# Conditioned residual stack on one core: the first eight turns of the first convolution in halves, a second queue for two transfers and a store, attention spread by row tiles

## The chip, the cores and the metric

One core of a Trainium2 chip. The time is the device time of one launch in microseconds (us), the median over runs; every run is the whole kernel. TensorE (PE) multiplies, ScalarE (ACT) and VectorE (DVE) work elementwise, GpSimd (POOL) copies, SyncE (SP) issues most of the transfers.

## What is computed

Four layers, each added to its input, on `x` of 32 samples x 128 channels x 2048 positions:

```python
x = x + conv9(x, weight0, groups=4, pad=4) + (c @ cw0.T)[:, :, None] + side[:, None]
x = x + einsum('boi,bih->boh', att1 @ experts1, x) + (att1 @ bias1)[:, :, None]
x = x + einsum('boi,bih->boh', att2 @ experts2, x) + (att2 @ bias2)[:, :, None]
x = x + conv9(x, weight3, groups=4, pad=4) + (c @ cw3.T)[:, :, None] + side[:, None]
# att = softmax(gelu(gelu(c @ W0 + b0) @ W1 + b1) @ W2 + b2), 8 experts of 128 x 128
```

## The kernel before

One sample at a time goes through three stages on TensorE. The two mixing layers have nothing nonlinear between them, so their two matrices are multiplied into one per sample (the *product*). A convolution over 2048 positions is laid out in four phases (`PH`) of 512 positions; with 9 taps this makes `SHIFTS` = 12 shifted products. Each fp32 value is split in a high and a low part in the matmul's own format, and three of the four partial products are summed, so a convolution has `TURNS` = 36 turns. A turn is four matmuls side by side (L836), one for each of the four groups of 32 channels, each in its own row tile of TensorE and with its own PSUM bank: turns 0 to 11 are high x high, 12 to 23 low taps, 24 to 35 low data. `conv0` is the first convolution, `mix` the mixing (12 turns, L906), `conv3` the last one, `product` the small matmul of the two matrices (L886, L893).

In the steady state, for each sample: ScalarE adds the bias and writes the high part (`high_y` L465, `high_z` L475), VectorE writes the low part (`low_y` L630, `low_z` L640), VectorE sums the expert matrices with the attention of the sample (`mix_matrices`, 16 instructions of L669), splits the product in `prod` (`split_product`, L677 to L682), and SyncE spreads it by four transfers of 32 partitions each to the four row blocks of `mix_w` (`spread_mix_w`, L326). GpSimd reorders the input and the output.

The order of the work on every engine is written out by hand; engines meet by semaphores only. The part that the change touches is the start and the end:

- **TensorE, start** (from L996 on). 12 filler matmuls (`keep_busy`, L998), the transpose of the condition (L1005), 4 fillers, the transpose of the five bias rows (L1008), 2 fillers, `hidden(0)` (L981: first MLP layer of both attentions), then `conv0(zero)` in groups of turns, and between the groups: `hidden(1)`, `logits` (L991, L992), transposes of the context weights (L1018), `mix2_transposes(0)` (L943: four expert matrices of the second mixer, to bank 4), `contexts` (L962), the attention's transposes (L1025), the broadcast of the attention of all samples to all partitions (L1030: a matmul of ones in 32 rows and a table `spread` of 32 x 512), `mix2_transposes(1)` to bank 5, the second mixer's attention bias (L1038), `conv_biases` (L969), the mixed bias in ten matmuls (`mixed_bias`, L955), the product of sample 0 after turn 24. Then turns 0 to 15 of the convolution of sample 1, and `mix(zero)`, which waits for all of `y_lo` and for the four transfers to `mix_w`.
- **ScalarE, start.** Six transfers (L550 to L554), the gelu table, the high parts of the taps (L489), the copy of the columns (L568), the gelus (L495), the exponentials (L574), the copies of the transposes (`mix2_transposed`, L500), the first planes of sample 1 (L455), the bias table (L590, L598), `high_y(zero)`.
- **VectorE, start.** Transpose of the taps (L689), high part of sample 0 (L771), low parts of the taps (L697), low part of sample 0 in pieces (`low_direct`, L621), softmax (L781 to L788), `spread` (L790), context columns (L751), copy of the attention table (L801), mixed terms (L805), the matrices.
- **The end.** The last sample's second convolution is done in two halves of 256 columns (`last_conv`, L874). VectorE transposes it to positions (L728, L731), VectorE or ScalarE adds the bias (L738, L533). ScalarE interleaves sample 30 (`weave_half`, L542). SyncE issues the stores of the last sample in eight pieces (L378) and that of sample 30 in two (L371), in the order: half 0 of groups 2, 3, 0, 1; the two of sample 30; half 1 of groups 0 to 3. A wait on SyncE holds all that stands behind it.

## Time and profile before

| | us |
|---|---|
| median of 3 runs (662.95 to 663.0) | 663.0 |
| the profiled execution | 663.23 |
| its span on the core | 661.4 |
| TensorE matmuls busy | 650.6 (98%) |
| VectorE busy | 476.5 (72%) |
| ScalarE busy | 262.3 (40%) |
| GpSimd busy | 241.7 (37%) |

The span runs from the first to the last recorded instruction; what the profiled execution has beyond it lies around it. An instruction on an engine starts when the one before it on the same engine has started and its semaphores allow it; a chain of waits is read backwards from the last instruction.

### The profile page before, as it was taken

The numbers are of one execution on the slowest core, as the hardware profiler recorded it, in microseconds if no ns is written. First come the engines' busy times: TensorE is split into PE (matmuls) and PEld (weight loads), VectorE is DVE, ScalarE is ACT, GpSimd is POOL, SyncE is SP. The second block draws the span as 40 slices with busy tenths as digits, with TensorE's granted clock in tenths as the row PEclk, the third lists the DMA queues.
The fourth block names the chain that finished last, engine by engine and source line by source line (L and its number), as shares of the span: only waits on it lengthen the run. The fifth ranks groups of instructions, "written<-read, shape, count | busy, mean of one in ns | idle before, by whom it ended". The sixth has DMA issues, their size and how long they took to land.

```text
span 661.4 us, 24661 instructions
## 1 busy us (share of the span) xinstructions
PE 650.6 (98%) x11220; PEld 595.9 (90%) x11220; DVE 476.5 (72%) x945; ACT 262.3 (40%) x328; POOL 241.7 (37%) x85
## 2 busy tenths in 40 slices
PE   8999999999999999999999999999999999999994
PEld 6889999999999999999999999999999999999994
DVE  7898867687767677677677677677677677677635
ACT  4643424433424433424433423433423433433434
POOL 3024334433424433434443433442433442433220
PEclk9999999999999999999999999999999999999998
DMA  7355776454566455566455566545566545444515
GB/s 235 97 162 161 224 224 213 155 175 183 168 222 219 153 168 191 159 222 222 156 163 194 154 222 222 165 153 199 150 223 223 164 154 205 153 154 161 159 67 192
DMA packets 50325, 118.77 MB, mean 180 GB/s; under 512 B 5557, under 2 KB 26090, under 8 KB 42474
## 3 DMA queue, kind: packets, MB, share of 16 engines
q1 hardware_dynamic: 49602, 117.48, 54.7%
q8 instruction: 28, 0.46, 0.3%
q10 hardware_dynamic: 488, 0.69, 0.3%
q14 instruction: 15, 0.12, 0.1%
q0 software_dynamic: 192, 0.02, 0.0%
HBM read 35.33 MB, written 33.55 MB: 104 GB/s over the span
## 4 chain that ended last, share of the span: by engine, by line
PE 96%; DVE 1%; DMA 1%; SPq 0%; ACTq 0%; ACT 0%; issue 0%
PE ps L836 79%; PE ps L906 14%; PE ps L893 1%; DMA out_planes<-in_L_cond_b 1%; PE ps L874 1%; DVE x_in L728 1%; DMA mix_w<-prod 1%; DVE x_planes L731 0%; PE ps L955 0%; SPq L326 0%; PE ps L943 0%; ACTq L554 0%; ACT x_planes L533 0%; PE ps L981 0%; PE ps L886 0%
## 5 line engine op out<-in xcount | busy, mean ns | idle before, releaser
L399 POOL COPY out_sb<-out_planes 128x2048 f32<-128x2048 f32 x30 | 118.7, 3956 | 220.4 <-DVE mat2T L669 208.4
L390 POOL COPY x_planes<-x_in 128x2048 f32<-128x2048 f32 x29 | 112.7, 3887 | 137.8 <-DVE x_lo L616 137.8
L465 ACT ACTIVATE y_hi<-ps,bias_tab 128x512 fp32r<-128x512 f32 x128 | 77.5, 689 | 189.1 <-PE ps L836 189.1
L640 DVE SCALAR_TENSOR_TENSOR z_lo<-ps,bias_tab,z_hi 128x1024 fp32r<-128x1024 f32 x62 | 76.8, 1280 | 69.2 <-ACT z_hi L475 69.2
L630 DVE SCALAR_TENSOR_TENSOR y_lo<-ps,bias_tab,y_hi 128x512 fp32r<-128x512 f32 x128 | 87.3, 745 | 38.9 <-ACT y_hi L465 38.9
L836 PE MATMUL ps<-z_hi,taps_lo 32*128 32x512 f32 x1488 | 99.4, 397 | 0.0
L836 PE MATMUL ps<-x_hi,taps_hi 32*128 32x512 f32 x1536 | 97.2, 391 | 0.0
L836 PE MATMUL ps<-x_hi,taps_lo 32*128 32x512 f32 x1536 | 96.5, 389 | 0.0
L836 PE MATMUL ps<-x_lo,taps_hi 32*128 32x512 f32 x1536 | 96.0, 390 | 0.0
L836 PE MATMUL ps<-z_hi,taps_hi 32*128 32x512 f32 x1488 | 92.9, 391 | 0.0
L483 ACT ACTIVATE out_taps<-ps,bias_tab 128x512 f32<-128x512 f32 x62 | 39.3, 684 | 134.3 <-PE ps L836 134.3
L836 PE MATMUL ps<-z_lo,taps_hi 32*128 32x512 f32 x1488 | 92.5, 390 | 0.0
L906 PE MATMUL ps<-y_hi,mix_w 32*128 32x512 f32 x1024 | 89.8, 389 | 0.3 <-DMA mix_w<-prod 0.3
L836 PEld LDWEIGHTS ps<-x_hi,taps_hi 32*128 32x128 f32 x1536 | 82.4, 184 | 7.1 <-issue 0.4
L836 PEld LDWEIGHTS ps<-x_lo,taps_hi 32*128 32x128 f32 x1536 | 82.2, 183 | 7.1
L836 PEld LDWEIGHTS ps<-x_hi,taps_lo 32*128 32x128 f32 x1536 | 82.4, 183 | 6.7 <-issue 0.2
L836 PEld LDWEIGHTS ps<-z_hi,taps_hi 32*128 32x128 f32 x1488 | 79.9, 183 | 7.0
L836 PEld LDWEIGHTS ps<-z_lo,taps_hi 32*128 32x128 f32 x1488 | 80.0, 183 | 6.7
L475 ACT ACTIVATE z_hi<-ps,bias_tab 128x1024 fp32r<-128x1024 f32 x62 | 65.7, 1112 | 50.0 <-PE ps L906 50.0
L836 PEld LDWEIGHTS ps<-z_hi,taps_lo 32*128 32x128 f32 x1488 | 77.0, 184 | 5.7
L616 DVE TENSOR_TENSOR x_lo<-x_planes,x_hi 128x2048 fp32r<-128x2048 f32 x31 | 70.8, 2284 | 0.0
L650 DVE TENSOR_SCALAR out_taps<-ps,bias_tab 128x512 f32<-128x512 f32 x62 | 43.7, 747 | 23.2 <-PE ps L836 23.2
(122 smaller groups left out, 554.2 us busy)
## 6 DMA issues: line engine op xcount, KB each, us to landing
x_in<-in_x SPq DMA_DIRECT2D x31, 1024.0 KB, 5.2
out_planes<-out_taps SPq DMA_DIRECT2D x122, 256.0 KB, 2.5
out<-out_sb SPq DMA_DIRECT2D x30, 1024.0 KB, 4.5
mix_w<-prod SPq DMA_DIRECT2D x128, 128.0 KB, 3.6
x_in<-in_x SPq DMA_DIRECT2D x2, 512.0 KB, 5.4
out<-x_planes SPq DMA_DIRECT2D x8, 128.0 KB, 2.1
out<-out_sb SPq DMA_DIRECT2D x2, 512.0 KB, 3.5
out_taps<-in_L_cond_weight SPq DMA_DIRECT2D x1, 512.0 KB, 6.5
```

What stands on the lines that cost most here:

```text
L390: pool.tensor_copy(x_planes[:, :, :], planes(x_in[t.par(d)], slice(0, S))).then_inc(x_planed, 1)
L399: pool.tensor_copy(out_sb[t.par(d)][:, :].rearrange("c (s p) -> c p s", p=PH), out_planes[:, :, :])\
L465: act.activation(y_hi[:, g, :], ps[:, bank(t, 0) + g, :], ACT.Identity, bias=bias_tab[:, b, g:g + 1]).then_inc(y_hi_done, 1)
L475: act.activation(z_home(t, 0)[0][:, 2 * h:2 * h + 2, 1:S + 1], ps[:, k:k + 2, :], ACT.Identity, bias=bias_tab[:, b, 2 * G:BIAS]).then_inc( ...
L483: act.activation(out_taps[:, g, :], ps[:, bank(t, d) + g, :], ACT.Identity, bias=bias_tab[:, b, G + g:G + g + 1]).then_inc(out_act, 1)
L616: dve.tensor_tensor(out=x_lo[p][:, :, 1:S + 1], in0=x_planes[:, :, :], in1=x_hi[p][:, :, 1:S + 1].bitcast(F32), op=ALU.subtract).then_inc( ...
L630: dve.scalar_tensor_tensor(out=y_lo[:, g, :], in0=ps[:, bank(t, 0) + g, :], scalar=bias_tab[:, b, g:g + 1], in1=y_hi[:, g, :].bitcast(F32) ...
L640: dve.scalar_tensor_tensor(out=z_home(t, 0)[1][:, 2 * h:2 * h + 2, 1:S + 1], in0=ps[:, k:k + 2, :], scalar=bias_tab[:, b, 2 * G:BIAS], in1 ...
L650: dve.tensor_scalar(out_taps[:, g, :], ps[:, bank(t, d) + g, :], bias_tab[:, b, G + g:G + g + 1], None, ALU.add).then_inc(out_dve, 1)
L728: dve.transpose(blocks(last_mid[:, h, g, :]), taps).then_inc(last_turned[h], 1)
L836: tile = pe.matmul(ps[:, first_bank + g, :], w[rows(g), d, :], a[rows(g), d % PH, d // PH:d // PH + S], start=(n == 0), stop=(n == TURNS - 1))
L906: tile = pe.matmul(ps[:, bank(t, 0) + p, :], w[rows(p), g, h, :], a[rows(p), g, :], start=(n == 0), stop=(n == 3 * G - 1))
```

## The change

- `half_turns(h, turns)` is new: a group of turns of the first convolution on 256 of the 512 columns. Turns 0 to 7 of sample 0 are done first for the left half (turns 0 and 1, then the transpose of the bias rows, then 2 to 7), which wait only for the left half of `x_hi` and for the taps of their own phase, then, behind `hidden(1)`, for the right half. Four filler matmuls go; the condition column and the bias columns get a copy and a semaphore each.
- The attention is computed on 128 partitions (each sample's logits four times over), both softmaxes share one reciprocal and one multiplication; `spread` has 128 x 128 elements, each block of 32 partitions with 8 samples of its own, and four matmuls of 128 columns, one for each row tile, write 128 columns each of banks 4 to 7. They wait for ScalarE's copy of bank 4. The attention's transpose moves from TensorE and ScalarE to VectorE. Both attention biases are one matmul (`MIXED` is 9).
- On TensorE the small matmuls stand at other places between the turns, the product of sample 0 comes after turn 33, and `mix(zero)` after 18 turns of sample 1.
- ScalarE issues two of the four transfers of sample 0's `mix_w` (`spread_first`), ahead of `high_y(zero)`; one of the four high tap copies of the last convolution moves behind `high_y(zero)`; the planes of sample 1 move behind the second transposes.
- At the end ScalarE issues the second half of sample 30 (`store_woven`), SyncE the first half, third in its line.

```diff
-MIXED = K + 2
+MIXED = K + 1
+SAMPLES = N // G
...
-        ones = sb("ones", [GC, C])
+        ones = sb("ones", [C, C])
+        own_samples = sb("own_samples", [C, SAMPLES])
...
-            spread_mix_w(zero, 0)
+
+            spread_mix_w(zero, 0, range(2))
             load_x(zero, 2)
...
+            store_group(0, 2)
+            store_group(0, 3)
+
+            sp.wait_ge(halves_woven, 1)
+            sp.dma_start(out[N - 2, :, 0:L // 2].rearrange("(g o) x -> o g x", g=G), out_sb[0][:, 0:L // 2])\
+              .then_inc(out_stored[0], DMA)
+            store_group(0, 0)
+            store_group(0, 1)
+            for g in range(G):
+                store_group(1, g)
...
+            def spread_first():
+
+                act.wait_ge(prod_hi_done, 1)
+                act.wait_ge(prod_lo_done, 1)
+                for p in range(2, PH):
+                    act.dma_start(mix_w[0][rows(p), :, :, :].rearrange("o g h z -> o g (h z)").bitcast(F32),
+                                  prod[:, :, :].rearrange("m h z -> m (h z)").bitcast(F32))\
+                       .then_inc(mix_w_spread[0], DMA)
...
+            def store_woven():
+
+                act.wait_ge(halves_woven, 2)
+                act.dma_start(out[N - 2, :, L // 2:L].rearrange("(g o) x -> o g x", g=G), out_sb[0][:, L // 2:L])\
+                   .then_inc(out_stored[0], DMA)
...
+            act.wait_ge(condT_psum, 1)
+            act.activation(condT, ps[:, 6, 0:N], ACT.Copy).then_inc(condT_done, 1)
             for p in range(PH):
                 taps_high(0, p)
-            act.wait_ge(condT_psum, 2)
-            act.activation(mlp_col[:, :], ps[:, 6, 0:N + 5], ACT.Copy).then_inc(condT_done, 1)
+            act.wait_ge(mlp_cols_psum, 1)
+            act.activation(mlp_col[:, N:N + 5], ps[:, 6, N:N + 5], ACT.Copy).then_inc(mlp_cols_done, 1)
             gelus(0)
             gelus(1)
...
             mix2_transposed(0)
-            act.wait_ge(attT_psum, 1)
-            act.activation(attT_sb[:, :, :], ps[0:K, 6, 256:320].rearrange("k (l n) -> k l n", l=2), ACT.Copy)\
-               .then_inc(attT_done, 1)
-            plane_x1(0)
             mix2_transposed(1)
             act.wait_ge(agg_psum, 1)
             act.activation(agg[:, :], ps[:, 6, 320:320 + N], ACT.Copy).then_inc(agg_done, 1)
+            plane_x1(0)
             plane_x1(1)
...
-            for p in range(PH):
+            for p in range(PH - 1):
                 taps_high(1, p)
...
             act.wait_ge(bias_tab_done, 3)
+            spread_first()
             high_y(zero)
+            taps_high(1, PH - 1)
             high_z(zero)
...
             weave_half(0)
             weave_half(1)
+            store_woven()
             bias_last()
...
-            turn_taps(1)
             dve.wait_ge(x_hi_done, 1)
-            low_direct(0, half(0), slice(0, 2), False)
+            low_direct(0, half(0), slice(0, 1))
+            low_direct(0, half(1), slice(0, 1))
             dve.wait_ge(logits_psum, 1)
...
+            turn_taps(1)
+            dve.wait_ge(exp_done, 2)
+            dve.reciprocal(att_inv, att_sum).then_inc(att_inv_done, 1)
...
+                              in0=att.rearrange("c (a k) -> c a k", a=1).to_broadcast([C, SAMPLES, ATT]),
+                              in1=own_samples[:, :].rearrange("c (m a) -> c m a", a=1).to_broadcast([C, SAMPLES, ATT]),
                               op=ALU.mult).then_inc(spread_done, 1)
...
+            dve.transpose(attT_sb[:, :], att_block).then_inc(attT_done, 1)
+            dve.wait_ge(att_tab_psum, G)
+            dve.tensor_copy(att_tab[:, :, :].rearrange("c (r m) k -> c r (m k)", r=G),
+                            ps[:, G:2 * G, 384:512]).then_inc(att_tab_done, 1)
+            for p in range(1, PH):
+                low_direct(0, half(0), slice(p, p + 1))
+                low_direct(0, half(1), slice(p, p + 1), p == PH - 1)
...
+            def half_turns(h, turns):
+
+
+                for n in turns:
+                    if h == 0:
+                        pe.wait_ge(x0_half_hi, 1)
+                        pe.wait_ge(taps_hi_done[0], min(n, PH - 1) + 1)
+                    else:
+                        pe.wait_ge(x_hi_done, 1)
+                    s = n // PH + HALF * h
+                    for g in range(G):
+                        pe.matmul(ps[:, g, HALF * h:HALF * h + HALF], taps_hi[0][rows(g), n, :],
+                                  x_hi[0][rows(g), n % PH, s:s + HALF], start=(n == 0 and h == 0), stop=False)
...
+            def spread_attention():
+
+                pe.wait_ge(spread_done, 1)
+                pe.wait_ge(mix2T_done, 1)
+                for r in range(G):
+                    pe.matmul(ps[:, G + r, 384:512], ones[rows(r), :], spread[rows(r), :, :].rearrange("n m k -> n (m k)"),
+                              start=True, stop=True).then_inc(att_tab_psum, 1)
...
-            keep_busy(4)
-            pe.wait_ge(mlp_rows_in, 5 * DMA)
-            pe.transpose(ps[:, 6, N:N + 5], mlp_rows, ident[0:5, 0:5]).then_inc(condT_psum, 1)
             keep_busy(2)
             hidden(0)
-            pe.wait_ge(taps_hi_done[0], PH)
-            conv0(zero, range(4))
+            half_turns(0, range(2))
+            pe.wait_ge(mlp_rows_in, 5 * DMA)
+            pe.transpose(ps[:, 6, N:N + 5], mlp_rows, ident[0:5, 0:5]).then_inc(mlp_cols_psum, 1)
+            half_turns(0, range(2, 8))
             hidden(1)
-            conv0(zero, range(4, 7))
+            half_turns(1, range(8))
             logits()
...
-            conv0(zero, range(7, 10))
+            conv0(zero, range(8, 11))
             mix2_transposes(0)
-            contexts()
...
+            spread_attention()
             conv0(zero, range(11, SHIFTS))
             pe.wait_ge(taps_lo_done[0], PH)
-            conv0(zero, range(SHIFTS, 14))
+            conv0(zero, range(SHIFTS, 15))
+            contexts()
             mix2_transposes(1)
...
+            conv0(zero, range(15, 19))
             conv_biases()
-            conv0(zero, range(14, 19))
+            conv0(zero, range(19, 25))
             for k in range(MIXED // 2):
                 mixed_bias(k)
-            conv0(zero, range(19, 25))
+            conv0(zero, range(25, 31))
             for k in range(MIXED // 2, MIXED):
                 mixed_bias(k)
+            conv0(zero, range(31, 34))
             product(zero, 0)
-            conv0(zero, range(25, TURNS))
+            conv0(zero, range(34, TURNS))
...
-            conv0(first, range(16))
+            conv0(first, range(18))
             mix(zero)
-            conv0(first, range(16, TURNS - 4))
+            conv0(first, range(18, TURNS - 4))
```

## Rows read from the trace of the kernel before

**Rows 1.** The page: TensorE's granted clock by slice; the ended-last chain by line.

```profile
PEclk9999999999999999999999999999999999999998
...
PE ps L836 79%; PE ps L906 14%; PE ps L893 1%; DMA out_planes<-in_L_cond_b 1%; PE ps L874 1%; DVE x_in L728 1%; DMA mix_w<-prod 1%; DVE x_planes L731 0%; PE ps L955 0%; SPq L326 0%; PE ps L943 0%; ACTq L554 0%; ACT x_planes L533 0%; PE ps L981 0%; PE ps L886 0%
```

**Rows 2.** The chain in order of time, steady part and last convolution: start, us, what.

```profile
83.63 4.20 PE ps L836 x72
...
644.26 4.30 PE ps L874 x143
```

**Rows 3.** The same chain, around the first mixing.

```profile
27.68 3.48 DMA mix_w<-prod
...
31.29 3.07 PE ps L906 x38
```

**Rows 4.** Timeline of TensorE, start: start, us, engine, line, count.

```profile
8.63 0.55 PE L981 MATMUL ps<-mlp_col,out_sb 128*128 128x32 f32 x4
9.11 1.22 PE L836 MATMUL ps<-x_hi,taps_hi 32*128 32x512 f32 x16
...
13.61 0.66 PE L943 MATMUL ps<-ident,out_taps 128*128 128x128 f32 x4
14.11 0.53 PE L962 MATMUL ps<-mlp_col,out_sb 128*128 128x32 f32 x4
...
15.06 0.69 PE L1030 MATMUL ps<-spread,ones 32*128 32x512 f32 x1
...
20.98 1.44 PE L836 MATMUL ps<-x_hi,taps_lo 32*128 32x512 f32 x20
...
22.58 0.85 PE L955 MATMUL ps<-out_sb,mix_wT 128*128 128x32 f32 x6
...
23.92 0.49 PE L886 MATMUL ps<-mat2T,mat 128*128 128x128 f32 x2
```

**Rows 5.** The line that issues the first MLP weights (L346), with its landing.

```profile
L346 SPq DMA_DIRECT2D out_sb<-in_L_cond_W x2: 432/521/610, 1.7 to 2.1; - x2
...
DMA to landing us min/median/max: 5.3/5.4/5.5
```

**Rows 6.** Timeline of the other engines, start, with the idle time before.

```profile
14.31 0.60 ACT L500 ACTIVATE mix_wT<-ps 128x512 f32<-128x512 f32 x1 [0.61 <-PE ps L943]
...
18.82 0.62 DVE L805 TENSOR_TENSOR out_sb<-agg,att_tab 128x256 f32<-128x256 f32 x1 [0.73 <-ACT agg L586]
...
25.03 0.29 DVE L682 TENSOR_TENSOR prod<-prod_sum,prod 128x128 fp32r<-128x128 f32 x1
...
25.41 2.87 SPq L326 DMA_DIRECT2D mix_w<-prod  x4
...
27.25 2.42 ACT L465 ACTIVATE y_hi<-ps,bias_tab 128x512 fp32r<-128x512 f32 x4 [2.15 <-PE ps L836]
28.04 2.73 DVE L630 SCALAR_TENSOR_TENSOR y_lo<-ps,bias_tab,y_hi 128x512 fp32r<-128x512 f32 x4 [0.61 <-ACT y_hi L465]
```

**Rows 7.** The line of the mix_w issues (L326), whole span: ns min/median/max.

```profile
L326 SPq DMA_DIRECT2D mix_w<-prod x128: 547/603/1748, 25.4 to 621.1; - x128
```

**Rows 8.** Timeline of the end: ScalarE and SyncE's issues.

```profile
645.90 1.45 ACTq L521 DMA_DIRECT2D out_planes<-out_taps  x2
...
650.38 3.93 ACT L542 ACTIVATE out_sb<-out_planes 128x1024 f32<-128x1024 f32 x2 [0.91 <-DMA out_planes<-out_taps]
...
652.16 2.53 SPq L378 DMA_DIRECT2D out<-x_planes  x4
...
654.52 0.96 ACT L533 ACTIVATE x_planes<-x_planes,bias_tab 128x256 f32<-128x256 f32 x2 [0.22 <-DVE x_planes L731]
654.74 1.25 SPq L371 DMA_DIRECT2D out<-out_sb  x2
...
656.03 3.34 SPq L378 DMA_DIRECT2D out<-x_planes  x4
656.39 0.96 ACT L533 ACTIVATE x_planes<-x_planes,bias_tab 128x256 f32<-128x256 f32 x2 [0.91 <-DVE x_planes L731]
```

146 lines of the change are left out of this document (74 added, 72 removed).

## Prediction, made before the changed kernel had run

> **What bounds the kernel now.** I read the page first: TensorE at its full clock in every slice but the last, and a chain that ended last which is convolution and mixing matmuls almost to the end [rows 1]. Then the chain in order of time. From about 32 us on it is one unbroken row of TensorE work: 18 turns (72 matmuls) take 4.20 us, 0.233 us a turn, and the turns of 256 columns of the last sample take 4.30 us for 36, 0.119 us each [rows 2]. Nothing of the change touches that middle. What it can move is when TensorE gets into that row, and what comes behind its last matmul. At the start the one piece of the chain that isn't TensorE's is the transfer of the first product to `mix_w`, issued at 27.68 and landed 3.48 us later; `mix(zero)` starts at 31.29 [rows 3]. Ahead of it TensorE is never idle for long, but a lot of its time goes to small matmuls between groups of turns [rows 4]. At the end SyncE issues ten stores in a row, the last four behind the woven sample's two [rows 8].
>
> **First convolution, start.** Now `hidden(0)` starts at 8.63 behind a wait for the five bias rows, and the turns at 9.11, 0.48 us later [rows 4]. In the change `hidden(0)` needs the condition column (cut loose from the bias rows) and its weights; these are issued up to 2.1 and land 5.3 to 5.5 us later, by 7.7 at the latest [rows 5]. The two turns after it need one half of `x_hi` only, which VectorE has by about then. So the turns start at about 7.7 + 0.05 + 0.48 = 8.2 us: 0.9 us earlier. The four filler matmuls that go lay in this wait and cost nothing; nothing else covered it.
>
> **From the first turn to the product.** Before: 9.11 to 23.92, 14.81 us [rows 4]. The change puts 34 turns ahead of the product where 25 stood: 9 x 0.233 = +2.10. The eight in halves cost 8 x (2 x 0.119 - 0.233), +0.04. A group of turns costs more than its turns: six turns from 20.98 to the next small matmul at 22.58 are 1.60 us where 6 x 0.233 = 1.40, and the small matmul ahead of a group waits some 0.08 more, so 0.28 a group. Seven groups (turns 0-3, 4-6, 7-9, 10, 11-13, 14-18, 19-24) become nine (first halves of 0-1 and of 2-7, second halves, 8-10, 11-14, 15-18, 19-24, 25-30, 31-33): +0.56. The transpose of the bias rows moves in: +0.15. Out go the attention row broadcast through one row tile (a pass of 512 columns shows 0.69 us, there are two, partly beside turns of other tiles; against four tiles of 128 columns side by side I take -0.8), the two attention transposes (-0.15) and one of ten matmul pairs of the mixed bias (six records from 22.58 last 0.85, so about -0.23 a pair) [rows 4]. And there is a **new wait**: the four tiles write to banks 4 to 7, bank 4 holds the first transposes of the second mixer, and ScalarE must have copied them. It started its copy 0.70 us after the transposes started and took 0.60 [rows 4, 6]; TensorE is through with the transposes after 0.50 (13.61 to 14.11) and has, in the new order, neither `contexts` nor the attention transposes to fill in. So it idles 0.70 + 0.60 + 0.05 - 0.50 = 0.85 us, with turns 11 to 14 queued behind. Sum: 14.81 + 2.10 + 0.04 + 0.56 + 0.15 - 1.18 + 0.85 = 17.33; the product starts at 8.2 + 17.3 = 25.5 us.
>
> VectorE isn't what the product waits for: its short softmax (two ops for four, a spread of 128 columns for 512) is done before ScalarE's copy is, it copies the table by 15.7, and with six low-part pieces and the context columns behind it reaches the mixed terms at about 19.4, where it stood at 18.82 before [rows 6]; the matrices are ready 4.8 us later, at 24.2, over a microsecond ahead of the product. Its additions at the start (two memsets, four small copies) lie in its wait for the taps. ScalarE's planes of sample 1 move behind the second transposes and end some 1 us later, with its bias column at about 25.6, just ahead of `conv0(first)`; no cost, but the cover is thin.
>
> **From the product to mix(zero).** Before, the product started at 23.92, its low part was done at 25.32, and SyncE issued the four spreads at 0.72 us each [rows 4, 6]. ScalarE's `y_hi` started at 27.25, and VectorE's last `y_lo` ended at 28.04 + 2.73 = 30.77, 3.52 later [rows 6]. In the change ScalarE issues two of the four, and it does so ahead of `high_y(zero)`: both issues count, `y_hi` is queued behind them, `y_lo` waits for `y_hi`, and `mix(zero)` waits for `y_lo`. With P for the product's start, the low part is at P + 1.40 and two issues of 0.72 end at P + 2.88. Then `y_hi` and `y_lo` take 3.52, and mix starts at P + 6.45 = 31.95. The two shorter lines of transfers land earlier than that: P + 1.49 + 0.87 + 3.5 = P + 5.85 (second issue, landing as in [rows 3]). TensorE itself arrives at P + 0.42 + 0.2 + 20 x 0.233 = P + 5.3, so it idles over a microsecond. Mix starts 31.95 - 31.29 = 0.66 us later than before, with two turns less behind it (-0.47): **start part +0.2 us**. The price of ScalarE's issues isn't shown for this transfer. The nearest row is its own pair at the end, 1.45 us for two [rows 8], and that I take. From below: if they delayed `y_hi` by nothing, the transfers decide, 31.35, and the start part is -0.4. From above: SyncE's longest of the 128 issues took 1.75 us [rows 7]; two such ones add 2.1.
>
> The Trainium skill speaks against splitting these transfers: by its page DMA: Bandwidth & Descriptors (Rules for kernel authors) transfers issued from two engines run on the same 16 DMA engines and nothing but issue time is saved. The trace has the last of the four landing 3.48 us after its own issue with three just ahead of it [rows 3], so issue time is what there is to save here; were it engine time, that would be the fourth rival.
>
> **The end.** Nothing before 652 us moves. SyncE's first four stores run 652.16 to 654.69, the woven pair to 655.99, the last four 656.03 to 659.37, which is 0.81 us more than the first four took [rows 8]. The bias of the last two groups is ready at 656.39 + 0.96 = 657.35, so the last issue could start 657.4, and it starts near 658.8. The change has SyncE issue one woven half third in line, and ScalarE the other after its weave ends at 650.38 + 3.93 = 654.31. ScalarE's first two biases then start 0.5 us later (655.05 for 654.52) and end near 656.0; SyncE issues group 0 at 655.6, 1 at 656.2, 2 at 656.9, 3 at 657.55. That is 1.2 us earlier. If the same 0.81 us of slow issues recurs, it is 0.45. With one store less on its queue I take **-1.0** (bounds -0.45 and -1.3). The third ending is none: were ScalarE's issue to take so long that its last biases slip, the gain would be gone.
>
> **Sum.** +0.2 - 1.0 = -0.8. The profiled execution took 663.23 us (span 661.4 and 1.8 around it) and would take 662.4. The median of the runs is 663.0, 0.2 below it, so the forecast is **662.2 us**, 0.12% less. What a measurement can tell from no change is 0.2%, 1.3 us; so this counts as within.
>
> **Rivals.**
> - *The start pays as well.* ScalarE's issues don't hold up `y_hi`, or the product comes earlier than 25.5 because TensorE's wait for the copy of bank 4 is shorter. Start -0.4, end -1.0: 661.6, just over 0.2% faster. For it: the turns do start 0.9 us earlier. Against: rows of ScalarE's queue show it busy for each issue. Chance 0.24.
> - *The end doesn't pay.* Slow issues recur, or ScalarE's issue delays its biases: end 0 to -0.45, start +0.2: 663.0, within. For it: the 0.81 us has no cause in the rows. Chance 0.18.
> - *ScalarE's issues are held like SyncE's slow ones.* Place: the two spreads ahead of `high_y(zero)`. At 1.5 to 1.75 us each the start part is +1.8 to +2.3; with the end at its lower bound that is +1.4 to +1.8, 664.4 to 664.8, say 664.6 us, slower by over 0.2%. It decides from about 1.5 us an issue. For it: `mix(zero)` has no slack against `y_lo`. Against: median of such issues 0.60 [rows 7], and nothing else loads the queue then. Chance 0.07.
> - *The split saves the transfers nothing.* The last one lands as long after the product's start as before (31.16 - 23.92 = 7.24 us), mix starts at 25.5 + 7.24 + 0.13 = 32.9, the start part is +1.1: 663.1, within. Against: the landing follows its issue by the same 3.5 us though the four came 0.75 us apart. By the skill's rule above it would be likelier than I make it. Chance 0.04.
> - *The forecast*, 0.47.
>
> **How the numbers follow.** The range takes the start from -0.4 (with 0.4 us of error on P on the good side) to +0.9, and the end from -1.3 to -0.45: 660.9 to 663.5; it leaves out most of the third rival and the far end of the first. Faster by over 0.2%: the first rival, 0.25 with the forecast's own edge; slower: 0.07; within: 0.68.
>
> **What would show it.** In the changed profile: `hidden(0)` near 7.8 and the first turns, 256 columns wide, near 8.2; TensorE idle 0.6 to 1.0 us ahead of the four spread matmuls, released by ScalarE's copy; the product near 25.5; two issues on ScalarE of about 0.7 us each, `y_hi` right behind them, and mix(zero) near 31.9 released by VectorE's `y_lo`; from there to the last matmul the same row of turns, shifted by +0.2; the last store issued within 0.3 us of the last bias. I am wrong if the last matmul ends over half a microsecond earlier than before, if mix(zero) is released by a transfer, or if the time from the last matmul to the end isn't about 1 us shorter.

## The result, and the profile after

The changed kernel takes **665.47 us**, the median of 10 runs (664.74 to 667.16); the kernel before beside it 663.13 (10 runs, 662.95 to 663.48). The ratio is 1.0039, interval 1.0031 to 1.0047: slower by 0.4%. The forecast was 662.2 within 660.9 to 663.5, so it is wrong in sign and outside its range. The profiled execution took 666.38 us with a span of 664.4; before, 663.23 and 661.4. In the traces the spans are 664.43 and 661.36, so they explain 3.07 of those 3.15 us.

TensorE at the start, timeline of the changed kernel (start, us, engine, line, count, and the idle time before it with what ended it). It answers to [rows 4]:

```profile
7.66 0.63 PE L1052 MATMUL ps<-mlp_col,out_sb 128*128 128x32 f32 x4 [0.32 <-DMA out_sb<-in_L_cond_W]
8.22 0.66 PE L906 MATMUL ps<-x_hi,taps_hi 32*128 32x256 f32 x9
...
14.63 0.46 PE L1073 MATMUL ps<-spread,ones 32*128 32x128 f32 x5 [0.78 <-ACT mix_wT L531]
...
25.45 0.49 PE L954 MATMUL ps<-mat2T,mat 128*128 128x128 f32 x2
...
32.72 0.50 PE L974 MATMUL ps<-y_hi,mix_w 32*128 32x512 f32 x4 [1.89 <-DMA mix_w<-prod]
```

Up to the product every step is where the working had put it: `hidden(0)` 7.66 (7.7 was said), turns 8.22 (8.2), a pause of 0.78 ahead of the spread attention (0.85), the product at 25.45 (25.5). Then `mix(zero)` starts at 32.72 for the 31.95 of the forecast, and what releases it is a transfer, not VectorE. TensorE stood still for 1.89 us. The other engines in that stretch, for [rows 6]:

```profile
26.97 1.60 ACTq L515 DMA_DIRECT2D mix_w<-prod  x2
28.62 2.42 ACT L483 ACTIVATE y_hi<-ps,bias_tab 128x512 fp32r<-128x512 f32 x4 [3.01 <-issue]
...
26.95 1.34 SPq L339 DMA_DIRECT2D mix_w<-prod  x2
...
29.42 2.73 DVE L669 SCALAR_TENSOR_TENSOR y_lo<-ps,bias_tab,y_hi 128x512 fp32r<-128x512 f32 x4 [0.46 <-ACT y_hi L483]
```

ScalarE's two issues take 1.60 us (1.44 was said), and `y_lo` is through at 29.42 + 2.73 = 32.15. So VectorE's line was read nearly right, 0.2 us late; the transfers' line was not. The chain in order of time (start, us, what), for [rows 3]:

```profile
27.70 4.88 DMA mix_w<-prod
32.72 4.62 PE ps L974 x44
```

The last spread, issued at 27.70, lands 4.88 us later, where the issue at 27.68 of the kernel before landed after 3.48. And the mixing behind it takes 4.62 us for 44 matmuls, where 38 took 3.07 before. The windows of this stretch say why (window, its length, busy time and count of PE, PEld, DVE, ACT and POOL, the granted clock, the busy share of the DMA engines, GB/s):

```profile
28.00:30.00 2.00, 2.00 (x43) 2.00 (x40) 1.54 (x5) 1.38 (x3) 0.00 (x0) 1.00 0.93 179
30.00:32.00 2.00, 0.82 (x16) 0.38 (x8) 2.00 (x4) 1.65 (x3) 0.00 (x0) 1.00 1.17 161
...
33.00:34.00 1.00, 1.00 (x16) 0.96 (x15) 1.00 (x1) 0.00 (x0) 0.00 (x0) 0.65 0.94 393
34.00:35.00 1.00, 1.00 (x16) 0.93 (x15) 1.00 (x4) 0.00 (x0) 0.00 (x0) 0.50 0.39 148
35.00:36.00 1.00, 1.00 (x16) 0.96 (x12) 1.00 (x5) 0.00 (x0) 0.00 (x0) 0.50 0.37 74
36.00:37.00 1.00, 1.00 (x19) 0.95 (x16) 0.44 (x2) 0.00 (x0) 0.00 (x0) 0.64 0.91 377
```

Two things are to be seen. While the four spreads run, the DMA engines are busy the whole time (0.93 and 1.17). And just behind the pause the granted clock falls to 0.50, the lower of TensorE's two levels, for 3.4 us. Before, that never happened ahead of the last matmul. In 3 of the 10 runs the mean granted clock is 0.993 where the others have 0.995 and above, and these three spans are 664.4 to 664.5 against 662.3 to 663.3. So the fall belongs to some executions, the profiled one among them.

The end, ScalarE and SyncE, for [rows 8]:

```profile
648.41 1.46 ACTq L552 DMA_DIRECT2D out_planes<-out_taps  x2
...
653.73 1.60 PE L942 MATMUL ps<-x_lo,taps_hi 32*128 32x256 f32 x48
...
654.67 1.24 SPq L385 DMA_DIRECT2D out<-x_planes  x2
654.84 3.87 ACT L573 ACTIVATE out_sb<-out_planes 128x1024 f32<-128x1024 f32 x2 [2.86 <-DMA out_planes<-out_taps]
...
656.92 0.54 SPq L392 DMA_DIRECT2D out<-out_sb  x1
...
657.50 4.94 SPq L385 DMA_DIRECT2D out<-x_planes  x6
...
658.73 0.62 ACTq L579 DMA_DIRECT2D out<-out_sb  x1
```

ScalarE's weave of sample 30 starts 6.43 us after the reload of that sample is issued; in [rows 8] it was 650.38 - 645.90 = 4.48. SyncE waits for the first half of it before its third store, so the line stands from 655.9 to 656.9, and the new order of stores, which was to end 1 us earlier, doesn't: from the start of the last matmul (655.06, before 652.56) to the end of the span it is 9.4 us, where it was 8.8.

**The ledger of the profiled execution**, from the start of the same matmuls in both traces. At `mix(zero)` +1.43 and, with two turns fewer behind it, -0.47: +0.96. The clock: +1.55, seen as a shift of 2.51 us of every mixing from the second to the last. Behind the last matmul +0.57. Outside the span +0.07 (1.95 for 1.88). Together 3.15. **The ledger of the medians** is another one: span +1.85 (663.05 for 661.2), and +0.5 outside the span, where the kernel before has 1.77 to 2.01 in every run whose span is on record, 1.9 in the median, and the changed one 1.84 to 2.92, median 2.41. So four things had to be tested: the wait for the transfers, the clock, the end, and the time outside the span.

### The profile page after: what moved, and what is told of

The parts are those of the page before. It is cut to its first block, busy times and chain, and to the rows that moved or that the text cites. A ratio compares the mean times of both kernels' runs of the same rounds, so it can differ in the third digit from the quotient of the medians.

```text
span 664.4 us, 24740 instructions
## 1 busy us (share of the span) xinstructions
PE 651.0 (98%) x11248; PEld 563.5 (85%) x11248; DVE 477.8 (72%) x954; ACT 262.7 (40%) x328; POOL 241.4 (36%) x85
## 4 chain that ended last, share of the span: by engine, by line
PE 95%; DMA 2%; ACT 1%; DVE 0%; SPq 0%; ACTq 0%; issue 0%; DVEq 0%
PE ps L890 79%; PE ps L974 14%; PE ps L961 1%; DMA out_planes<-out_taps 1%; DMA out_sb<-in_L_cond_W 1%; DMA mix_w<-prod 1%; ACT out_sb L573 1%; PE ps L906 0%; PE ps L1025 0%; ACT x_planes L564 0%; PE ps L1052 0%; DVE out_taps L689 0%; PE ps L1013 0%; PE ps L954 0%; SPq L356 0%
## 5 line engine op out<-in xcount | busy, mean ns | idle before, releaser
L890 PE MATMUL ps<-x_hi,taps_hi 32*128 32x512 f32 x1504 | 93.3, 390 | 0.0
L890 PEld LDWEIGHTS ps<-x_lo,taps_hi 32*128 32x128 f32 x1536 | 77.6, 183 | 11.6
L890 PEld LDWEIGHTS ps<-x_hi,taps_lo 32*128 32x128 f32 x1536 | 77.7, 183 | 11.0
L890 PEld LDWEIGHTS ps<-x_hi,taps_hi 32*128 32x128 f32 x1504 | 76.1, 184 | 11.4 <-issue 0.3
L890 PEld LDWEIGHTS ps<-z_hi,taps_hi 32*128 32x128 f32 x1488 | 75.0, 183 | 11.9
L890 PEld LDWEIGHTS ps<-z_lo,taps_hi 32*128 32x128 f32 x1488 | 75.1, 183 | 11.7
L890 PEld LDWEIGHTS ps<-z_hi,taps_lo 32*128 32x128 f32 x1488 | 72.4, 184 | 9.9
L974 PEld LDWEIGHTS ps<-y_hi,mix_w 32*128 32x128 f32 x1024 | 52.4, 185 | 10.5 <-DVE y_lo L669 2.3
```

The lines of the kernel that those rows point to most:

```text
L890: tile = pe.matmul(ps[:, first_bank + g, :], w[rows(g), d, :], a[rows(g), d % PH, d // PH:d // PH + S], start=(n == 0), stop=(n == TURNS - 1))
L974: tile = pe.matmul(ps[:, bank(t, 0) + p, :], w[rows(p), g, h, :], a[rows(p), g, :], start=(n == 0), stop=(n == 3 * G - 1))
```

## Experiments: the wait for the transfers

**All four spreads by SyncE** (`a_sp4`), the changed kernel with one part undone.

```diff
-            spread_mix_w(zero, 0, range(2))
+            spread_mix_w(zero, 0)
...
-            spread_first()
             high_y(zero)
```

> The changed kernel with all four spreads of sample 0 issued by SyncE again, none by ScalarE. Theory (the four transfers are limited by the DMA engines at about 0.9 us each, whoever issues them): the last lands at 32.5 to 32.9, mix(zero) starts at 32.7 to 33.0, no more than 0.3 us later than with two issuers, though y_hi starts 1.5 us earlier; time 665.4 to 665.8. Rival (issue time counts, as the prediction had it): each issue of 0.72 us more on one queue lands later, mix(zero) at 34.1, time 667. Rival 2 (ScalarE's issues hold y_hi and that is what costs): mix(zero) near 31.4, time 664.

665.57 us (7 runs), ratio 1.0032 (1.0021 to 1.0043): nothing won, nothing lost. In its trace `mix_w` by SyncE (issues: count, ns min/median/max; then the time to landing), and the first mixing:

```profile
L339 SPq DMA_DIRECT2D mix_w<-prod x4: 602/602/702, 27.0 to 29.0; - x4
...
DMA to landing us min/median/max: 3.1/3.4/3.6
...
32.75 0.65 PE L973 MATMUL ps<-y_hi,mix_w 32*128 32x512 f32 x4 [1.82 <-DMA mix_w<-prod]
```

The last spread is issued 1.3 us later than in the changed kernel and lands at the same 32.6; `y_lo`, no longer behind ScalarE's issues, ends at 31.6, and mixing starts at the same time. So issue time was not what the landing hung on: the later the issue, the shorter the time to landing (3.6 us here for 4.88).

**The same from the other side** (`b_act2`): the kernel before, with ScalarE issuing two of the four spreads, and nothing else.

```diff
+            def spread_first():
...
-            spread_mix_w(zero, 0)
+            spread_mix_w(zero, 0, range(2))
...
+            spread_first()
             high_y(zero)
```

> The kernel before with two of the four spreads of sample 0 issued by ScalarE ahead of high_y(zero), nothing else. Theory (the transfers are limited by the DMA engines at 0.9 us each): the last lands within 0.3 us of 31.16, mix(zero) at 31.1 to 31.3; ScalarE's issues end near 27.1, ahead of its y_hi at 27.25, so they cost nothing: 663.3. Rival (issue time counts): mix(zero) at 30.8, held by y_lo, 662.8.

663.09 us (11 runs), ratio 1.0000 (0.9991 to 1.0009). The product starts at 24.19 and mixing at 31.32, 7.13 later. The last spread is issued at 26.43, 1.25 us earlier than in the kernel before, and lands at 31.18, where it landed at 31.16.

**Less work ahead of the product** (`a_prod`): the changed kernel with the product right behind the mixed bias, after turn 30.

```diff
-            conv0(zero, range(31, 34))
             product(zero, 0)
-            conv0(zero, range(34, TURNS))
+            conv0(zero, range(31, TURNS))
```

> The changed kernel with the product of sample 0 right behind the mixed bias, turns 31 to 33 behind it. Theory (mix(zero) starts 7.27 us after the product): the matrices are ready at 24.7, product at 24.7, mix(zero) at 32.0, TensorE's pause 1.2 us; if so short a pause leaves the clock alone, 0.75 + 1.55 us less, 663.2; if the clock still falls, 664.7. Rival (mix(zero) is held by y_lo, which hangs on ScalarE's issues): mix(zero) moves by under 0.3 us.

664.86 us (11 runs), ratio 1.0023 (1.0014 to 1.0032), 0.6 below the changed kernel. Its product starts at 24.84, 0.61 earlier, and mixing at 32.18 behind a pause of 1.23 instead of 1.89; in none of its 11 runs did the clock fall (lowest mean 0.995). I had expected 663.2: its span is 662.3 in the median, and 2.55 us lie outside it.

**More work ahead of it** (`b_late`): the kernel before with the product after turn 33 and 18 turns ahead of `mix(zero)`, as in the change, and no other part of it.

```diff
-            product(zero, 0)
-            conv0(zero, range(25, TURNS))
+            conv0(zero, range(25, 34))
+            product(zero, 0)
+            conv0(zero, range(34, TURNS))
...
-            conv0(first, range(16))
+            conv0(first, range(18))
             mix(zero)
```

> The kernel before with one thing of the change alone: the product of sample 0 after turn 33 instead of 24, and 18 turns of sample 1 ahead of mix(zero) instead of 16. Theory (the four spreads land 7.2 us after the product's start, whatever else): product at 23.92 + 9 x 0.233 + about 0.2 = 26.2, mix(zero) at 33.4 to 33.6 after a pause of 2.7 us, the clock falls for 3.4 us behind it; 2.2 - 0.5 later by the wait, 1.6 by the clock: time 663.3 + 3.3 = 666.6. Without a fall of the clock 665.0. Rival (the place of the product is harmless, the loss sits in the new attention or in the halves): under 664.

665.11 us (5 runs), ratio 1.0042 (1.0028 to 1.0055). This one move makes the kernel before as slow as the changed one. Product 26.03, mixing 33.34, a pause of 1.85, and in 2 of 5 runs the mean clock is 0.993. I had expected a pause of 2.7 us and the fall in every run, 666.6.

Over all these kernels one number holds. From the start of the product to the start of mixing it is 7.37 us before, 7.27 in the change, 7.34 (`a_prod`), 7.31 (`b_late`), 7.13 (`b_act2`), 7.29 (`a_sp4`), whoever issues. What moves mixing is when the product starts. The Trainium skill's page DMA: Bandwidth & Descriptors (Rules for kernel authors) says that spreading transfers over issuing engines saves only time of issue, since they all run on the same 16 DMA engines. Here the traces agree: by one issuer or by two, the last landing is 7.0 to 7.3 us behind the product's start. One profiled execution stands apart: the changed kernel with the old end (`a_noend`, below) has its spreads landed within 3.9 us of their issues, and mixing 6.47 after the product, held by `y_lo`. Its packets of 1 KB take 88 ns each from 29 to 31 us, where those of the changed kernel take 124 to 128; why, I can't say. So 7.3 is what the transfers take in most executions, and VectorE's line, at 6.4 to 6.7 in the changed kernel, is the bound right behind it.

## Experiments: the pause and the clock

**Filling the pause with nothing** (`a_fill`): eight turns of matmuls with zero weights, which add zero to banks that are being summed, ahead of `mix(zero)`; SyncE, ScalarE and VectorE do what they did.

```diff
             conv0(first, range(18))
+            add_zeros(8)
             mix(zero)
```

> The changed kernel with eight turns of matmuls with zero weights, 1.87 us, ahead of mix(zero), added to the banks of sample 1 (adds zeros, so nothing of the result changes); they fill TensorE's wait for mix_w. Theory (the pause drops the clock): mix(zero) starts where it did, 32.7, the clock stays full in all slices, and the product of sample 1 starts near 39.0 instead of 40.59; time 1.5 us below the changed kernel's, about 664. Rival (the clock falls for another reason, fewer fillers at the start or the 0.8 us pause ahead of the attention spread): the clock still falls for 3.4 us near 33 and the time stays at 665.5.

**Filling it with work** (`a_24`): 24 turns of sample 1 ahead of `mix(zero)` instead of 18.

```diff
-            conv0(first, range(18))
+            conv0(first, range(24))
             mix(zero)
-            conv0(first, range(18, TURNS - 4))
+            conv0(first, range(24, TURNS - 4))
```

> The changed kernel with 24 turns of sample 1 ahead of mix(zero) instead of 18: the same work, six turns (1.4 us) moved into the wait. Theory: TensorE's pause shrinks from 1.9 to 0.5 us, mix(zero) starts at 32.7, six turns less stand behind it, and the clock stays full: product of sample 1 near 39.0 - 1.4 = 37.6, time about 665.5 - 1.5 - 1.4 = 662.6. Rival (what stands behind the moved turns, z and the next mix, is the bound): mix(zero) and all after it stay where they are and only the pause moves behind, time 664 to 665.5.

`a_fill`: 664.49 us (11 runs), ratio 1.0019 (1.0010 to 1.0028). `a_24`: 664.91 us (11 runs), 1.0022 (1.0013 to 1.0031). They mix at 32.76 and 32.75, like the changed kernel, and in none of their 22 runs did the clock fall. The windows of `a_fill` at the place where the changed kernel showed 0.65, 0.50 and 0.50:

```profile
33.00:34.00 1.00, 1.00 (x21) 0.97 (x21) 1.00 (x1) 0.00 (x0) 0.00 (x0) 1.00 0.94 393
34.00:35.00 1.00, 1.00 (x24) 0.98 (x20) 1.00 (x4) 0.00 (x0) 0.00 (x0) 1.00 0.39 148
35.00:36.00 1.00, 1.00 (x24) 0.98 (x20) 1.00 (x5) 0.08 (x1) 0.00 (x0) 1.00 0.54 66
```

21 and 24 matmuls in a microsecond for 16. In the changed kernel the next product starts at 40.52, in `a_fill` at 39.06: the 1.5 us of the clock. Eight turns that compute nothing make the profiled execution faster by 1.9 us. Of the 1.0 us between the medians the span has only 0.35 (663.05 and 662.7), for the clock fell in 3 of 10 runs; the rest lies outside it. With real work in the pause TensorE gains another 0.6 us at the last matmul (`a_24`: +0.46 against the kernel before, `a_fill` +1.05), but its median doesn't show it, because it has 1.84 to 2.98 us outside the span (median 2.64) where `a_fill` has 1.8 in each run. More on that below. I had expected 1.4 us from the six moved turns; in the trace TensorE then waits 0.80 us for VectorE's `z_lo` ahead of the product of sample 1, at 38.50, which takes back more than half of it.

**The fillers put back** (`a_kb`): the changed kernel with six for two ahead of `hidden(0)`.

```diff
-            keep_busy(2)
+            keep_busy(6)
             hidden(0)
```

> The changed kernel with the four filler matmuls put back ahead of hidden(0). Theory (the fall of the clock near 33 hangs on the pause ahead of mix(zero) alone and comes in some runs and not in others): hidden(0) about 0.3 us later, nothing else moves, 665.5, some runs 1.5 us above the others as in the changed kernel. Rival (the fillers kept the clock up): no run with a mean clock of 0.993, 664.9.

666.69 us (6 runs), ratio 1.0049 (1.0035 to 1.0062). `hidden(0)` starts at 8.39 instead of 7.66, the product at 26.07, and mixing at 33.38 behind a pause of 1.95; in 5 of 6 runs the clock fell. So fillers at 6 us don't protect it at 33. And they were not free: of the 0.97 us by which `hidden(0)` came earlier, 0.73 is theirs.

Taken together: a pause of 1.8 to 1.95 us ahead of `mix(zero)` cost the clock in 3 of 10, 2 of 7, 2 of 5 and 5 of 6 runs; one of 1.23 us in none of 11; one of 0.5 or none in none of 22. (`a_noend` has 1.1 us in its profiled execution and the clock fell in 2 of its 9 runs; those two aren't the profiled one, so how long they paused isn't known. `a_trim`, below, pauses 1.88 us in its profiled execution and the clock stays up behind it; it had fallen and risen again before, between 12.6 and 16.1 us.)

## Experiments: halves alone, the end alone, and together

**Only the halves** (`b_half`): the kernel before with its own softmax and spread, eight turns in halves, the four fillers gone, the product after turn 25 and the small matmuls placed between the turns accordingly.

```diff
-            keep_busy(4)
...
             keep_busy(2)
             hidden(0)
-            conv0(zero, range(4))
+            half_turns(0, range(2))
...
+            half_turns(0, range(2, 8))
             hidden(1)
-            conv0(zero, range(4, 7))
+            half_turns(1, range(8))
             logits()
```

> The kernel before with the start of the change alone: turns 0 to 7 of sample 0 in halves, the bias rows' transpose between them, four fillers fewer; attention, product place (behind the mixed bias, now turn 26) and end as before. Theory: the first turns start at 8.2 instead of 9.1, but TensorE waits for VectorE's attention table and mixed terms, so the product starts where it did, 23.7 to 23.9, and mix(zero) at 31.2: time 663.2, no gain. Rival (the prediction's sum: 0.9 us earlier is 0.9 us earlier): product at 23.2, mix(zero) at 30.6, 662.5.

663.68 us (11 runs), ratio 1.0009 (1.0000 to 1.0018). Here I had expected too little of the start: the product starts at 23.31, mixing at 30.61, and every mixing is 0.68 us earlier than before, for the whole run. The time doesn't show it. The weave starts 6.4 us after the reload's issue, TensorE stands still inside the last convolution (0.15 us ahead at its last matmul where it was 0.68 ahead, so 0.5 us lost), and the time outside the span is 2.60 in the median. The late weave and the time outside are those of the changed kernel, whose end part isn't in this one; the stop of TensorE is not in the changed kernel's profiled execution, but it is in that of `a_sp4` and `a_prod`.

**Only the end** (`b_end`), and **only the end undone** (`a_noend`).

```diff
+            store_group(0, 2)
+            store_group(0, 3)
+            sp.wait_ge(halves_woven, 1)
...
             weave_half(1)
+            store_woven()
             bias_last()
```

> The kernel before with the end part of the change alone (SyncE stores the first half of sample 30 third in its line, ScalarE the second half behind its weave). Prediction's theory: the last store is issued 0.45 to 1.3 us earlier, time 662.1 (-1.0). Rival (SyncE now waits for the weave with the stores of groups 0 and 1 behind that wait, and ScalarE's issue delays its biases): 0, time 663.1, or slower by up to 0.5 in runs where the relay lands late.

> The changed kernel with the end of the kernel before (SyncE stores both halves of sample 30 behind the first half of sample 31, ScalarE none). Theory: the end part is worth 0.6 us as in the kernel before, so this is 0.6 us slower than the changed kernel, near 666.1. Rival: in the changed kernel the relay of sample 30 lands 1.7 to 2 us late, its weave holds SyncE's line, and the new order of stores is what suffers from it: this one is equal or faster, 665 to 665.5.

`b_end`: 662.73 us (11 runs), ratio 0.9990 (0.9981 to 0.9999), 0.6 us less than the kernel before beside it. The slow issues recur (SyncE's 0.78, 1.05 and 0.75 us among nine); it is the lower bound of the forecast's end, not its -1.0. `a_noend`: 665.37 us (9 runs), 1.0033 (1.0022 to 1.0044): in the changed kernel the end part is worth nothing that can be measured. The line of stores there waits for a weave that is 2 us late in any order.

**Two reworked kernels.** `b_18end` is the kernel before with two edits: 18 turns ahead of `mix(zero)`, and the end. `best1` is the changed kernel with SyncE's issues, the product behind the mixed bias after turn 29, 22 turns ahead of mixing, and parts of VectorE's and ScalarE's start reordered.

```diff
-            conv0(first, range(16))
+            conv0(first, range(18))
             mix(zero)
```

> A version for both sides of the kernel before: 18 turns of sample 1 ahead of mix(zero) instead of 16, and the end of the change; no more. Theory: TensorE's wait of 0.5 us ahead of mix(zero) is filled with two turns that then don't stand behind it, last convolution of sample 0 at 39.0 for 39.46; with the end part 0.5 + 0.6: 662.2. Rival (the chain over z binds): -0.6, as the end part alone, 662.7.

```diff
-            conv0(zero, range(25, 31))
+            conv0(zero, range(25, 30))
             for k in range(MIXED // 2, MIXED):
                 mixed_bias(k)
-            conv0(zero, range(31, 34))
             product(zero, 0)
-            conv0(zero, range(34, TURNS))
+            conv0(zero, range(30, TURNS))
...
-            conv0(first, range(18))
+            conv0(first, range(22))
             mix(zero)
```

> A version meant to be faster than both: the changed kernel with SyncE issuing all four spreads; the attention spread behind three turns, so that TensorE doesn't pause for bank 4; one low-part piece of VectorE ahead of the attention table, so that the matrices are ready at 23.5; the product behind the mixed bias after turn 29; 22 turns of sample 1 ahead of mix(zero); the product of sample 1 split ahead of the low taps; the end as in the change. Theory: product at 23.6, mix(zero) at 30.9 with a pause under 0.3 us, last convolution of sample 0 near 37.7 (39.46 in the kernel before): -1.7 at the start, -0.6 at the end, 661.0; with the relay landing late as in the changed kernel 661.6. Rival (the chain from mix(zero) over z or the next mix_w binds): -0.5 at the start, 662.3.

`b_18end`: **662.15 us** (11 runs), ratio 0.9988 (0.9979 to 0.9997): 1.0 us below the kernel before, both parts where they were expected. `best1`: 663.76 us (11 runs), 1.0014 (1.0005 to 1.0023), although TensorE is 0.85 us ahead at its last matmul and the median span is 661.0, 0.1 below the kernel before beside it: 2.76 us lie outside it. I had expected 661.0 to 661.6, with the product at 23.6; it starts at 24.19 behind a wait of 0.41 us for VectorE's matrix. Three of its 11 spans are 662.6 to 662.7 with a mean clock of 0.995 to 0.997, and that is unexplained.

## Experiments: the late reload and the time outside the span

What separated the kernels so far was no part of the change. It was the length of TensorE's compiled program. All kernels with both the reload on time and 1.8 to 2.0 us outside have 471744 bytes (the kernel before, `b_end`, `b_act2`, `b_late`, `b_18end`). Those with 475776 to 475968 (`b_half`, the changed kernel, `a_sp4`, `a_24`, `a_prod`, `a_noend`, `best1`) have a late reload and up to 3.0 outside; `a_fill`, with 480064, and `a_kb`, with 476480, have the late reload alone (`a_kb` 1.8 to 2.2 outside). These are the lengths of the compiled programs, not figures of a trace. The traces show a queue of the kind "instruction" with 28 or 29 transfers of 16384 bytes over the run; 29 of them are 475136. Six kernels tried this.

`a_trim`: the changed kernel with six turns in halves for eight, 474816 bytes.

```diff
-            half_turns(0, range(2, 8))
+            half_turns(0, range(2, 6))
             hidden(1)
-            half_turns(1, range(8))
+            half_turns(1, range(6))
...
-            conv0(zero, range(8, 11))
+            conv0(zero, range(6, 11))
```

> The changed kernel with six turns of the first convolution in halves for eight; turns 6 and 7 whole, behind the logits. TensorE's program is 474816 bytes long, below 29 pieces of 16384 (475136); the changed kernel's is 475968. If the length of the program is what costs: the time outside the span is back at 1.8 to 2.0 us in every run (changed kernel 1.84 to 2.92, median 2.41), the reload of sample 30 lands about 4.5 us after its issue, and the median is some 0.6 to 1.2 us lower, 664.3 to 664.9. If the order of the work costs: outside median 2.4 or more, the reload again 6 us after its issue, 665.4. The start is the same by both: product near 25.5, mix(zero) near 32.7, the clock fallen behind it in some runs.

664.98 us (8 runs), ratio 1.0025 (1.0015 to 1.0035), 0.5 below the changed kernel, with 1.92 to 2.0 outside the span in every run. The late reload stays, with a TensorE pause of 0.7 us beside it. What I had not expected is at the start: with two half turns fewer TensorE waits 0.36 us ahead of `hidden(1)`, and in the profiled execution the clock falls already at 12.6 us, so that the product starts at 27.21.

`b_pad` and `b_pad2`: the kernel before with waits that hold nothing, behind its last matmul (475968 bytes); the second with 32 more small matmuls among the fillers (480064).

```diff
             for h in range(2):
                 last_conv(h)
+            for i in range(130):
+                pe.wait_ge(zeros_done, 1)
```

> The kernel before with 130 waits behind TensorE's last matmul, on a semaphore that has long been reached; they hold nothing. TensorE's program grows from 471744 to 475968 bytes, the changed kernel's length. If the length costs: the time outside the span rises from 1.8 to a median above 2.3, and the reload at the end is late; the median is 663.6 to 664.2, above the kernel before by 0.4 to 1.0. If the order of the work in the changed kernels is what costs: as the kernel before in everything, 663.1, outside 1.8 to 2.0.

```diff
-            keep_busy(12)
+            keep_busy(8)
+            for i in range(36):
+                pe.matmul(ps[:, i % G, 0:32], y_hi[:, 0, 0:C], y_hi[:, 0, 0:32], start=True, stop=True)
```

> As b_pad, and 32 more small matmuls among the fillers at the start, where TensorE waits for its inputs anyway: 480064 bytes, further beyond the boundary. If what costs outside the span is a last piece with only a few instructions in it: outside back at 1.8 to 2.0 although the program is longer, while the reload may still be late; 663.1 to 663.6. If each byte beyond the boundary costs: outside as in b_pad or more, 663.8 or above. If the length has no effect: 663.1.

`b_pad`: 663.82 us (11 runs), ratio 1.0011 (1.0002 to 1.0019). Outside 1.78 to 1.86, reload on time: length alone, put there, does neither. (Its 0.7 us are in the span, among slower store issues; I can't name their cause.) `b_pad2`: 678.73 us (6 runs, 671.5 to 685.1). It is no measure of length: its 36 matmuls of 32 columns stand for four of the fillers, and behind them the clock is at 0.5 from 8.6 to 32.5 us in the profiled execution. (In three of the runs, 671.5 and the two longest, the mean clock is 0.995 or more, so the clock alone doesn't explain its times.) But its reload is late and `b_pad`'s is not, and what the second adds is at the start.

`b_shift` therefore changes nothing but the place: 132 waits on a semaphore long reached, among the first twelve fillers, and no work moved.

```diff
-            keep_busy(12)
+            for i in range(12):
+                keep_busy(1)
+                for j in range(11):
+                    pe.wait_ge(zeros_done, 1)
```

> The kernel before with 132 waits on a semaphore long reached spread among its first twelve fillers. No other work is changed; TensorE's program grows from 471744 to 475584 bytes, all of it ahead of the first convolution, so that the pieces of 16384 bytes are cut 3840 bytes earlier in all the code behind. If the place of the cuts is what makes the reload of sample 30 late: its weave starts 6 us or more after the issue (4.5 in the kernel before), TensorE may pause 0.3 to 0.7 us in the last convolution, and with 448 bytes in the last piece the time outside the span has a median above 2.2; 663.6 to 664.4. If the moved work of the changed kernels is what makes it late: 4.5 us after the issue, no pause, outside 1.9 or (by the length alone) above; 663.1 to 663.7.

665.08 us (5 runs), ratio 1.0035 (1.0022 to 1.0049). The waits themselves slow the fillers, and everything to the last convolution is 1.42 us later. But the end also changes, timeline of ScalarE and of TensorE's weight loads:

```profile
653.78 3.86 ACT L542 ACTIVATE out_sb<-out_planes 128x1024 f32<-128x1024 f32 x2 [2.88 <-DMA out_planes<-out_taps]
...
652.52 0.68 PEld L874 LDWEIGHTS ps<-x_lo,taps_hi 32*128 32x128 f32 x19
653.56 1.00 PEld L874 LDWEIGHTS ps<-x_lo,taps_hi 32*128 32x128 f32 x29 [0.36 <-issue]
```

The same in `b_pad`, where the same waits stand behind the last matmul:

```profile
645.64 1.46 ACTq L521 DMA_DIRECT2D out_planes<-out_taps  x2
...
650.27 3.93 ACT L542 ACTIVATE out_sb<-out_planes 128x1024 f32<-128x1024 f32 x2 [1.06 <-DMA out_planes<-out_taps]
```

With the padding ahead the weave starts 6.45 us after the reload's issue at 647.33, as in the changed kernel, and TensorE stands still for 0.4 us with no semaphore that it waits for; with it behind, 4.63 and no pause. And the time outside the span is 2.07 to 2.11 in three runs and 3.18 and 3.30 in two. So both go with where the pieces of the program are cut in the code of the end, and not with the work that the change moves. In `b_shift`, `b_half`, `best2` and `a_trim` ScalarE's weave and TensorE's restart come within 0.3 us of each other, as if one thing released both. The transfers that carry the program come close to being it. These are the DMA queues in the last reload, the kernel before from 650.0 to 651.0 and the changed one from 651.6 to 652.6 (queue, kind: packets, MB, share of the 16 engines), and one window of the changed kernel behind that:

```profile
q8 instruction: 1, 0.02, 6.6%
q10 hardware_dynamic: 1, 0.00, 0.0%
...
q10 hardware_dynamic: 119, 0.21, 58.2%
q1 hardware_dynamic: 43, 0.06, 17.0%
q8 instruction: 1, 0.02, 5.8%
...
653.00:654.00 1.00, 1.00 (x44) 1.00 (x40) 1.00 (x4) 0.00 (x0) 0.00 (x0) 1.00 0.05 18
```

In the kernel before the piece of program is fetched at 650.08, when the last packet of the reload has started. In the changed kernel it is fetched at 651.64, in the middle of the reload: 168 packets of the reload start after it, the last of them trickle at 18 GB/s and less, and the reload lands at 654.82. This parts all the kernels. In the seven with the reload on time (the kernel before, `b_end`, `b_act2`, `b_18end`, `b_late`, `b_pad`, `best3`) no packet of the reload starts after the fetch, and in the thirteen with a late one at least one does, 1 in `best2` and 2 in `a_trim`. So a late reload goes with a fetch that falls into it; that its last packets stand behind the fetch on one DMA engine would explain it, but the rows don't show which engine a packet took. TensorE's stop goes with the same fetch: in the eight kernels that have one it restarts 2.2 to 2.5 us after the fetch starts (`b_shift`: 651.15 and 653.56), as it would if it needed that piece.

The fetches also sort the time outside the span. In the five profiled executions with 2.56 to 3.0 us outside (`b_half`, `a_sp4`, `a_24`, `a_prod`, `best1`) one more piece is fetched 1.8 to 2.0 us after the span has ended, and in the other fifteen, with 1.8 to 2.1 outside, none is. The changed kernel's profiled execution is one of the fifteen (1.95); its runs with 2.4 and more weren't profiled.

**Putting the paying parts together.** `best2` is `b_half` with six turns in halves (474624 bytes), 18 turns ahead of mixing, and the end part; `best3` has four turns in halves (473472 bytes).

> The kernel before with its own softmax, its product after turn 25 and its transfers by SyncE; six turns of the first convolution in halves, the four fillers gone, 18 turns ahead of mix(zero) for 16, and the stores of the end as in the change. TensorE's program is 474624 bytes, below the boundary. If the parts add up: -0.7 for the halves, -0.3 to -0.5 for the two turns, -0.6 for the end against the kernel before: 661.3 to 661.6, outside 1.8 to 2.0. If the clock falls behind the longer lead, or the halves bring the late reload with them: 662.2 or above.

```diff
-            half_turns(0, range(2, 6))
+            half_turns(0, range(2, 4))
             hidden(1)
-            half_turns(1, range(6))
+            half_turns(1, range(4))
...
-            conv0(zero, range(6, 11))
+            conv0(zero, range(4, 11))
```

> best2 with four turns in halves for six (1152 bytes less at the start; 473472 in all, 1728 more than the kernel before). The start is as in best2 or up to 0.2 us later, since two half turns fewer cover the wait for the right half of x_hi. If a shift of the cuts of this size is small enough for the reload to be on time, without the pause of TensorE at the end: 661.4 to 661.8, below best2 (662.15) and the kernel before. If it isn't: 662.1 to 662.4.

`best2`: 662.15 us (11 runs), ratio 0.9992 (0.9983 to 1.0002). TensorE is 0.89 us ahead up to the last convolution, the time outside is back at 1.8, but the reload is late and a pause costs most of it (and in 3 of the 11 runs the mean clock is lower):

```profile
651.63 3.87 ACT L550 ACTIVATE out_sb<-out_planes 128x1024 f32<-128x1024 f32 x2 [3.04 <-DMA out_planes<-out_taps]
...
651.82 0.77 PEld L907 LDWEIGHTS ps<-x_lo,taps_hi 32*128 32x128 f32 x21 [0.70 <-issue]
```

`best3`: 663.56 us (11 runs), ratio 1.0003 (0.9993 to 1.0013). Its reload is on time (4.73 us) as hoped, though its weight loads still pause for 0.29 us, 2.3 us after the fetch; but its start fails: four half turns don't cover `hidden(1)`, TensorE waits 0.60 us, and the clock falls at 11 us in the profiled execution; 7 of 11 runs have a lower mean clock.

```profile
9.34 0.60 PE L1014 MATMUL ps<-out_sb 128*128 128x32 f32 x4 [0.60 <-ACT out_sb L503]
...
10.00:12.00 2.00, 1.90 (x28) 1.30 (x28) 1.90 (x5) 1.94 (x4) 0.00 (x0) 0.78 1.19 321
12.00:14.00 2.00, 2.00 (x21) 1.63 (x24) 1.90 (x9) 0.91 (x6) 0.00 (x0) 0.50 0.98 405
```

So the fastest of all is `b_18end`, which takes two small parts of the change and leaves the rest, with `best2` at the same median.

## Why the prediction was wrong

**First convolution, start** ("the turns start at 8.2 us: 0.9 us earlier"): right in its number, at 8.22, wrong in its reason. I put the whole gain on the wait for the bias rows and priced the fillers at nothing; `a_kb` shows that they carry 0.73 of it.

**From the first turn to the product** ("the product starts at 25.5 us"): right, 25.45, with the new wait of 0.78 and the terms for groups of turns. VectorE's last matrix ends at 24.68, half a microsecond later than the 24.2 worked out, and still ahead of the product.

**From the product to mix(zero)**: this step failed first. I put the last landing at P + 5.85 by taking the time from issue to landing as fixed at 3.5 us, and named as bound `y_lo` at P + 6.45. The last landing is at 32.58, P + 7.1, and mixing at P + 7.27. The row I leaned on, 3.48 us after its issue, fits a queue that is always full as well as one that is never full; `a_sp4` tells them apart. The fourth rival had this step right, at 32.9 against 32.72 measured, and I gave it 0.04; its total, 663.1, missed too, since it knew neither the clock nor the end. Its start part was +1.1, and the trace has +0.96 without the clock. It is the one that the Trainium skill's rule spoke for. ScalarE's issues, on which the third rival stood, were harmless: 0.80 us each. That mix(zero) is released by a transfer was one of the signs of being wrong that the prediction had named, and so was an end that isn't 1 us shorter.

**What no step of it held: the clock.** TensorE's arrival at P + 5.3 was worked out, and so a pause of over a microsecond was accepted at the price of its length. It became 1.89, and in 3 of 10 runs the clock fell behind it, +1.55 us in the profiled one. `a_fill` and `a_24` show that it goes with the pause.

**The end** ("I take -1.0 (bounds -0.45 and -1.3)"): mis-sized. Alone it measured -0.6 (`b_end`); my second rival had its slow issues. In the changed kernel the late reload gives that back (`a_noend` against the changed kernel: 0.1 us). "Nothing before 652 us moves" was wrong in this one place: the reload lands 2 us later after its issue, and the weave starts 6.43 us behind it for 4.48.

**"Its span and what lies around it"**: I took the 1.8 us around the span as given. It is 2.41 in the median after, and 1.96 in `a_trim`, whose edit changes only two turns in halves for two whole ones.

The sum by what was measured: +0.96 for the start, some 0.5 for the clock as a mean over runs (3 of 10 times 1.55), +0.57 behind the last matmul (-0.5 from the order of the stores and +1.07 from the late reload), +0.5 outside: 2.5, where the means differ by 2.54 and the medians by 2.34.

What stays open: that the fetch itself holds the reload and TensorE, and that the late fetch is the time outside, is read from when they happen and wasn't tested apart. That they go with the place of the cuts is shown by `b_shift` alone of the kernels in which no work was moved; its 5 runs are few. Nor do the runs show why the clock falls behind such a pause in some executions and not in others.

## What to carry to other kernels

Before splitting transfers between queues, ask what the last landing counts from: here 7.3 us from the product whoever issued, so only an earlier product helps. Price a pause of TensorE by its length and by the clock that may fall behind it; work of no use in that place can keep it up (`a_fill`: no fall in 11 runs). And when a change lengthens a long unrolled program, compare the time outside the span, the last transfers and the moments at which the program's pieces are fetched as well: the same waits made the last reload 2 us late when they stood ahead of the first turn, and not when they stood behind the last matmul.
